# Routed layers: GpSimd makes the low parts of the first four weight pieces during the routing, VectorE's share of the first group is four pieces smaller

## The reference

```python
def _L1_ffn_ref(x, Wg, W1, W2, W3):
    gate_out = jnp.einsum('bsd,ed->bse', x, Wg)
    top_v, top_i = jax.lax.top_k(gate_out, K)          # K = 2
    probs = jax.nn.softmax(top_v, axis=-1)
    out = jnp.zeros_like(x)
    for e in range(E):                                 # E = 8, hidden width 1024
        w_e = jnp.sum(probs * (top_i == e), axis=-1)
        h1 = jnp.einsum('bsd,hd->bsh', x, W1[e])
        h2 = jnp.einsum('bsd,hd->bsh', x, W2[e])
        g = h1 * jax.nn.sigmoid(h1) * h2
        y = jnp.einsum('bsh,dh->bsd', g, W3[e])
        out = out + y * w_e[..., None]
    return out
```

## Time and profile before

| | us |
|---|---|
| median of 3 runs | 1998.14 |
| lowest, highest run | 1996.32, 2005.67 |
| profiled execution, its own time | 1994.87 |
| its span in the profile | 1993.1 |

### The profile page before, as it was taken

How to read it: one execution, slowest core, us unless ns; L and a number is a source line. 1 busy time by engine, 2 the same in 40 slices (tenths; PEclk the granted TensorE clock), 3 DMA queues, 4 the chain that set the end, 5 groups by cost and what they waited for, 6 DMA issues and landing times. The chain is left out here.

```text
span 1993.1 us, 35333 instructions
## 1 busy us (share of the span) xinstructions
PE 1887.8 (95%) x12196; PEld 1550.4 (78%) x12196; DVE 1016.9 (51%) x2218; ACT 867.5 (44%) x1811; POOL 588.1 (30%) x490
## 2 busy tenths in 40 slices
PE   7999999999999999999699999999998967999994
PEld 6788787878878787878478888888885747999994
DVE  7446565646565555545543333233346755554664
ACT  5344444435444444444433334333324433555651
POOL 1010101010010101000135554355521104788883
PEclk9999999999999999999799999999999977999997
DMA  8722121121211121110433333233367044555646
GB/s 307 284 65 85 31 70 42 39 81 39 81 35 59 35 85 35 37 61 13 143 96 113 114 112 126 61 101 111 116 216 260 18 145 124 181 172 163 212 155 216
DMA packets 121393, 221.31 MB, mean 111 GB/s; under 512 B 31779, under 2 KB 38083, under 8 KB 120735
## 3 DMA queue, kind: packets, MB, share of 16 engines
q1 hardware_dynamic: 116447, 203.68, 31.1%
q0 software_dynamic: 4800, 15.73, 2.4%
HBM read 190.56 MB, written 28.41 MB: 110 GB/s over the span
## 5 line engine op out<-in xcount | busy, mean ns | idle before, releaser
L566 POOL TENSOR_TENSOR a_kvin_raw<-a_kvin_raw,a_rows 128x722 f32<-128x722 f32 x32 | 57.9, 1842 | 562.9 <-DMA a_rows<-a_norm_dram 562.9
L772 PE MATMUL a_kv_ps<-a_kvin_hi,a_wk_hi 128*128 128x512 f32 (+1 forms) x512 | 190.1, 371 | 2.0 <-DVE a_qs_lo L1057 2.0
L1288 PE MATMUL f_banks<-f_wab_hi,f_x_hi 128*128 x448 | 185.4, 414 | 1.3 <-DVE f_x_lo L2018 1.1
L774 PE MATMUL a_kv_ps<-a_kvin_hi,a_wk_lo 128*128 128x512 f32 (+1 forms) x512 | 179.6, 351 | 0.0
L773 PE MATMUL a_kv_ps<-a_kvin_lo,a_wk_hi 128*128 128x512 f32 (+1 forms) x512 | 178.9, 349 | 0.0
L1290 PE MATMUL f_banks<-f_wab_hi,f_x_lo 128*128 x448 | 176.9, 395 | 0.0
L1289 PE MATMUL f_banks<-f_wab_lo,f_x_hi 128*128 x448 | 175.7, 392 | 0.0
L1751 ACT ACTIVATE f_h_sb<-f_banks 128x256 f32<-128x256 f32 x112 | 43.0, 384 | 297.6 <-PE f_banks L1290 292.4
L2040 DVE TENSOR_TENSOR f_h_sb<-f_h_sb,f_banks 128x256 f32<-128x256 f32 x112 | 47.2, 421 | 244.4 <-ACT f_h_sb L1751 243.4
L637 ACT ACTIVATE a_probs_t<-a_t_ps 128x500 f32<-128x500 f32 x128 | 74.9, 585 | 190.8 <-PE a_t_ps L871 190.8
L1288 PE MATMUL m_banks<-m_wab_hi,m_x_hi 128*128 x512 | 155.7, 304 | 2.3 <-DVE m_x_lo L2018 1.7
(11 more groups left out here) (457 smaller groups left out, 4793.7 us busy)
## 6 DMA issues: line engine op xcount, KB each, us to landing
f_raw<-f_pieces SPq DMA_DIRECT2D x94, 256.0 KB, 2.7
m_raw<-m_pieces SPq DMA_DIRECT2D x92, 256.0 KB, 3.0
f_wab_raw<-f_pieces SPq DMA_DIRECT2D x42, 512.0 KB, 6.0
m_wab_raw<-m_pieces SPq DMA_DIRECT2D x42, 512.0 KB, 6.2
a_kvin_raw<-a_ctx_t SPq DMA_DIRECT2D x8, 1444.0 KB
a_rows<-ctx SPq DMA_DIRECT2D x8, 1280.0 KB
a_rows<-a_norm_dram SPq DMA_DIRECT2D x8, 722.0 KB
a_wout_sb<-L_xattn_Wkv SPq DMA_DIRECT2D x8, 512.0 KB, 11.2
```

Source lines behind the costliest of these rows:

```text
L566: nc.gpsimd.tensor_tensor(x, x, spread_norm[:, :, 0], ALU.subtract).then_inc(scaled_done, 1)
L772: nc.tensor.matmul(out, hi_l, hi_r, start=first, stop=False)
L774: return nc.tensor.matmul(out, lo_l, hi_r, start=False, stop=last)
L1288: nc.tensor.matmul(out, left_hi, right_hi, start=start, stop=False)
```

## The change

In both routed layers the low parts of pieces 0 to 3 of group 0 (`SPARE` = 4) go from VectorE to GpSimd, which makes them ahead of its wait for `rows_at`, as soon as their high parts are there. VectorE's four splits under TensorE's row matmuls are now of pieces 4 to 7, and its splits after the first gather are of pieces 8 to 15, so there are 8 instead of 12. The tokens' low parts still stand after the 4th and the 6th. The counts in the waits are shifted accordingly, and each slot of TensorE's first group gets a wait on `wlo_pool` as well.

```diff
+    SPARE = 4
...
-        H0, LO0, ADD0, LOW0 = 2, 2, 4, 1
+        H0, LO0, ADD0, LOW0 = 2, 2, 4, 1 + SPARE
...
-            return g == 0 and c < LAST or g == G - 1 and c >= PIECES - SHARED
+            return g == 0 and SPARE <= c < LAST or g == G - 1 and c >= PIECES - SHARED
...
-        POOL_FIRST = PIECES - LAST
+        POOL_FIRST = SPARE + PIECES - LAST
...
+            low_weights(0, 0, SPARE)
             pool.wait_ge(rows_done, 1)
             gather_rows(0)
             pool.wait_ge(expert_done, 2)
             used = pool.value_load(expert[0:1, SLOTS:SLOTS + 1], min_val=0, max_val=SLOTS)
-            low_weights(0, 0, G * PIECES)
+            low_weights(0, SPARE, G * PIECES)
...
-                        pe.wait_ge(wlo_dve[q], LOW0 + PER + PER * experts[s])
+                        pe.wait_ge(wlo_pool[q], LOW0 + SPARE)
+                        pe.wait_ge(wlo_dve[q], LOW0 - SPARE + PER + PER * experts[s])
...
-            for c in range(AHEAD):
+            for c in range(SPARE, SPARE + AHEAD):
                 split(0, 0, c)
...
-            for c in range(AHEAD, LAST):
+            for c in range(SPARE + AHEAD, LAST):
                 split(0, 0, c)
-                if c == AHEAD + 3:
+                if c == SPARE + AHEAD + 3:
                     low_tokens(0, 0)
-                if c == AHEAD + 5:
+                if c == SPARE + AHEAD + 5:
                     low_tokens(0, 1)
```

## The result

| us | before | after |
|---|---|---|
| median | 1996.98 (20 runs) | 2005.78 (20 runs) |
| lowest, highest run | 1991.06, 2005.67 | 1996.16, 2012.78 |
| profiled execution, its own time | 1994.87 | 2012.06 |
| its span | 1993.1 | 2010.3 |

The ratio is 1.004 with an interval of 1.0026 to 1.0054: 5 to 11 us slower, under what I called tellable (10 us), but past zero. The medians are 8.8 us apart and the two profiled executions 17.2. This gap between the two differences became half of the study.

What follows compares the result with a forecast made beforehand. TensorE bounds the kernel, but each routing is bound by VectorE's serial chain of small instructions. Delays of 3.7 + 3.7 = 7.4 us, less a gain of 0, on a median of 1998.14 gave 2005 us, range 1997 to 2010.

Steps and rivals of the forecast that it cites:

- GpSimd's own stream, 0: GpSimd's four subtractions per layer run in its idle time before the list and delay no gather by themselves: 0.
- The chain in f, +3.7 (up to 4.1): f's routing: four VectorE instructions each wait out a GpSimd subtraction; +3.7 us, +4.1 if L1964's second is caught too.
- The chain in m, +3.7: m's routing: same waits, first at L1946, fourth at L1954 if small scalings wait, +3.7 us; if not, +2.7.
- VectorE's smaller share, gain 0: Behind the first gather: 2.5 us less VectorE work per layer, waited for again at the second silu; 0, at most 2.7.
- From the profiled time to the median, +7.4 on either: Whole kernel: +7.4 us takes the profile from 1994.87 to 2002.3; the median lies 3.3 us above the profiled one.
- swallowed delay: Rival: chain late by 7.4 us, but the second silu still starts at 1006.8 and 1671.9; 1998 +- 1, chance 0.15.
- faster: Rival: small VectorE instructions slip between GpSimd's in the routing, no delay and 2.7 us won; 1995.4, chance 0.07.
- half: Rival: chain late as forecast, but in m the silu or another wait takes back its part; +3.7, 2002, chance 0.12.
- The sign that I had named for the swallowed case: First gather to second silu should stay at 19.7 and 22.9 us; shrunk by the delay, the swallowed case holds.
- Slower by over 10 us: Rival: the whole routing chain stands still during GpSimd's four, PSUM instructions and reductions too; 11 us, 2009, chance 0.08.

Runs made afterwards that it cites:

- pace_after: The changed kernel, but in m's last group GpSimd's low parts wait for VectorE's so the two take turns; 2005.03 us, ratio 1.0024 to the kernel before.
- look_after: The changed kernel, unchanged, profiled once more; one run, 1988.5 us.
- late: The changed kernel with turns in m's last group, GpSimd's four subtractions held until VectorE's chain ends (`at_row` done); 2000.19 us in one run.
- look_before: The kernel before, unchanged, profiled once more; one run, 1994.94 us.
- f_only: The changed kernel with the four pieces moved to GpSimd in layer f alone, none in m; 1998.91 us, ratio 1.0007 to the kernel before.
- fill_only: The kernel before with four GpSimd fills of zeros in each routing where the moved subtractions would stand; 2001.31 us, ratio 1.0017.

## Why the prediction was right

The forecast was 2005, the measured median 2005.8. That the totals are so close is partly luck: the three runs that I started from had a median 1.2 us over that of twenty (1998.14 and 1996.98), and the step of 7.4 us was 1.4 smaller than the measured 8.8. By its own steps:

- **GpSimd's own stream, 0: right.** Its four ran in idle time, and the wait for the list fell to 9.64 us where I had worked out about 10.
- **The chain in f, +3.7 (up to 4.1): right in mechanism, 0.15 too large.** 3.55 us in the profile. The four instructions are the third of the group of three and the three named ones, all with grown lengths. The fourth ends at 981.93, with GpSimd's last at 981.91, where I had let it only start then. In pace_after it was 4.09 us to the first gather. There GpSimd started 0.3 us earlier, and all three of the group were caught (the line is L1969 in that kernel), so that the four were these and the next. My 4.1 has nearly the same price, but stood for another four, the second of the group to L1969 of before. The rows are VectorE's timeline in pace_after:

```profile
976.72 3.73 DVE L1969 TENSOR_TENSOR f_scratch<-f_scratch 128x32 f32<-128x32 f32 x3
980.48 1.19 DVE L1971 TENSOR_TENSOR f_scratch<-f_scratch 128x28 f32<-128x28 f32 x1
981.70 0.18 DVE L1973 TENSOR_REDUCE f_scratch<-f_scratch 128x4 f32<-128x28 f32 x1
981.91 0.17 DVE L1974 TENSOR_TENSOR f_scratch<-f_scratch 128x16 f32<-128x16 f32 x1
```

- **The chain in m, +3.7: right on the scalings, 0.3 too large.** GpSimd began some 0.3 us earlier against the chain than I had set it, so that the first to be caught was the scaling L1946 (L1943 before the change), and then came one two-input instruction and two more scalings, L1950 and L1953 of before. In look_after and pace_after, where GpSimd began 0.2 and 0.4 us later against the first fill, the four are those of the prediction, L1946, L1950, L1953 and L1954, and the first gather is later by 3.50 and 3.67 us. The prediction's count passes over L1951 without a reason: it is a scaling too and was caught in none of these, and it starts before L1950 has ended. L1954 does the same behind L1953 and is caught in two of the three. That small scalings wait as the long one of the earlier trace rows does was the choice on which 3.7 instead of 2.7 rested, and three rows of 0.95 to 1.16 us bear it out.
- **VectorE's smaller share, gain 0: held in the sum, for a wrong reason.** From the first gather to group 1 the first pair differs by +0.3 in f and +0.2 in m, so nothing was won. But I had said that the second silu is tied to the gathers. `late` refutes it: the gathers were 4.3 us later, and the silu came 16.8 and 15.2 us after the first of them; in m the unnamed wait had moved on to the third silu. So do look_before and look_after, with 13.1 us in m. The stretch has a wait of its own, of 8 to 10 us in m, that some executions have and others don't, and against it a share of 2.5 us can't be seen. Between these two, after is 4.0 us shorter there than before in m and 1.1 in f. Whether that is the share's gain or the switch I can't say; one pair does not tell it, and the medians (8.4 to 8.9 us apart in three pairs, against a chain of 7.0 to 7.8) speak against a gain of 2.7 us, though with intervals of some 3 us to each side they don't exclude it. What the medians have over the chain, 0.7 to 1.8 us, is within these intervals and stays unexplained.
- **From the profiled time to the median, +7.4 on either: right for the median, wrong for the profile.** The step took one execution as standing for the kernel but for a fixed 3.3 us to the median. The profiled execution of after came out 9.8 us over the 2002.3 that I gave, by the long low part of m's last group. For the sign of each stretch the profile could be trusted, for its total not.

The rivals: swallowed delay, faster and half fall with the first gather, which is late by 7.0 us or more in every pair, with the medians further apart than that and not less. The sign that I had named for the swallowed case is absent too: from the first gather to the second silu it is 20.1 and 23.0 us after the change, against 19.7 and 22.9. Slower by over 10 us falls with the reductions and the copies from PSUM, which kept their lengths in both layers (0.17 and 0.18 us for the reductions of f, 0.28 for the copy L1952 of m).

## What to carry to other kernels

Idle time of GpSimd beside a serial chain of short VectorE instructions is not free: each GpSimd instruction that reads SBUF can hold up one link of the chain for its whole length, and one that only fills can still hold up a scaling, so count the subtractions, not the overlap, and price them at one GpSimd instruction less the link itself. Beside VectorE's long splits it was no cheaper: there GpSimd was the one shut out, and the gathers came 4.3 us later. What I would try next, and did not run, is such work beside VectorE instructions that read PSUM or reduce one input, which kept their lengths here, or at a place where nobody waits for either engine. And where the totals of two profiles differ by more than the change can explain, cut both spans at the same instructions before looking for a cause: here the change sat in two stretches of 3.5 us, and 9.9 us lay in one that it never touched.

## What was not expected of the hardware

- A VectorE subtraction of 128 x 512, 0.68 us alone, either takes turns with GpSimd's (1.37 us) or is shut out by it for as long as GpSimd's run goes on, 8.56 to 8.58 us over seven of its subtractions, in four of the six traces of kernels without turns or gap (after, f_only, fill_only, look_before); nothing between the two was seen for these subtractions. In `late` it is GpSimd that is shut out, 3.45 us behind four of VectorE's. I had taken turns as the rule, from the earlier trace rows alone. What decides it is open. A wait of GpSimd on its own last result went with turns both times.
- ScalarE's second silu in m stands 22.9 or 13.1 us behind the first gather in two executions of the kernel before, 23.0 or 13.1 in two of the kernel after, 15.2 in `late` and 22.6 to 22.9 in the others; in f it is 14.9 to 20.1 over all of them. The cause is open: in before's profile ScalarE is idle there for 8.1 us with a releaser that is not in the records.
- Four fills of GpSimd that read nothing delayed m's chain, where they met scalings, by 2.0 us, and f's, where they met mostly two-input instructions, by 0.4.
